# Decoder layer on one core: the recurrence's work in another order on all engines, and TensorE's program written out instead of looped

## What is computed

```python
q, k, v = (x @ Wq), (x @ Wk), (x @ Wv)          # each (b, s, H, HD)
fg = jax.nn.sigmoid(x @ Wf + bf)
def step(state, inp):
    qt, kt, vt, gt = inp
    state = state * gt[..., None] + vt[..., None] * kt[..., None, :]
    out_t = jnp.einsum('bhij,bhj->bhi', state, qt)
    return (state, out_t)
_, outs = jax.lax.scan(step, state0, (qs, ks_, vs, gs))
```

## Time and profile before

| | |
|---|---|
| median of 3 runs | 2022.22 us (2022.18 to 2028.58) |
| the profiled execution | 2018.74 us, span 2016.6 us |
| TensorE products, busy | 1864.5 us (92%), 28151 |
| TensorE weight loads, busy | 1307.0 us (65%), 28151 |
| VectorE, busy | 1593.3 us (79%) |
| ScalarE, busy | 1221.4 us (61%) |
| GpSimd, busy | 390.4 us (19%) |
| instruction DMA (queue 8) | 162 packets, 2.65 MB |

### The profile page before, as it was taken

How to read it: one execution, slowest core, us unless ns; L and a number is a source line. 1 busy time by engine, 2 the same in 40 slices (tenths; PEclk the granted TensorE clock), 3 DMA queues, 4 the chain that set the end, 5 groups by cost and what they waited for, 6 DMA issues and landing times. The chain is left out here.

```text
span 2016.6 us, 71020 instructions
## 1 busy us (share of the span) xinstructions
PE 1864.5 (92%) x28151; PEld 1307.0 (65%) x28151; DVE 1593.3 (79%) x2870; ACT 1221.4 (61%) x2047; POOL 390.4 (19%) x516
## 2 busy tenths in 40 slices
PE   6999999999999977999999999999599988799798
PEld 4666666666666665888888888887344433344687
DVE  6777777777777775888888888887466799998897
ACT  4444554444445434777777777777355666688565
POOL 1111111211111121223232323232100222100121
PEclk9999999999999989999999999999699999999899
DMA  4001100110011001111111111110188788599574
GB/s 126 24 24 29 30 24 24 29 30 24 24 27 32 19 19 63 34 48 32 46 33 46 36 42 38 40 41 7 40 273 267 272 314 312 188 402 409 184 271 148
DMA packets 121324, 205.24 MB, mean 102 GB/s; under 512 B 44851, under 2 KB 98358, under 8 KB 121142
## 3 DMA queue, kind: packets, MB, share of 16 engines
q1 hardware_dynamic: 121142, 202.43, 29.4%
HBM read 108.01 MB, written 85.98 MB: 96 GB/s over the span
## 5 line engine op out<-in xcount | busy, mean ns | idle before, releaser
L1483 PE MATMUL ff_twin<-ff_xq,w_uh 128*128 (+1 forms) x1152 | 346.0, 382 | 40.0 <-DVE ff_top L1852 25.7
L1483 PEld LDWEIGHTS ff_twin<-ff_xq,w_uh 128*128 128x128 f16 x1152 | 110.4, 98 | 188.9 <-issue 43.2
L1483 PE MATMUL ff_twin<-ff_xq,w_ul 128*128 (+1 forms) x576 | 219.9, 382 | 0.0
L1214 DVE TENSOR_REDUCE mneg<-att_s 128x4 f32<-128x512 f32 x256 | 158.8, 683 | 31.3 <-PE att_s L977 31.3
L545 ACT ACTIVATE x<-rec_e,rec_hidden 128x512 f32<-128x512 f32 x256 | 155.8, 702 | 35.1 <-PE rec_e L380 35.1
L661 DVE TENSOR_TENSOR x<-rec_x,rec_until 128x512 f32<-128x512 f32 x256 | 158.7, 681 | 17.2 <-PE rec_x L364 17.2
L392 PE MATMUL rec_x<-x 32*32 32x64 f32 x8192 | 146.4, 219 | 14.9 <-DVE x L661 9.5
L392 PEld LDWEIGHTS rec_x<-x 32*32 32x32 f32 x8192 | 125.4, 107 | 51.4 <-issue 51.3
L288 POOL TENSOR_TENSOR rec_o<-rec_tmp 128x512 f32<-128x512 f32 x32 | 41.1, 1283 | 571.6 <-DVE rec_tmp L714 571.6
L1129 ACT ACTIVATE att_e<-att_s 128x512 f32<-128x512 f32 x256 | 132.2, 612 | 25.4 <-PE att_s L1011 25.4
L349 PE MATMUL rec_f<-rec_xT,w_rec 128*128 128x256 f32 x512 | 137.3, 402 | 0.8 <-ACT rec_v L527 0.8
(11 more groups left out here) (244 smaller groups left out, 4363.3 us busy)
## 6 DMA issues: line engine op xcount, KB each, us to landing
raw_scratch<-ff_out SPq DMA_DIRECT2D x32, 768.0 KB, 3.5
ff_in<-raw_scratch SPq DMA_DIRECT2D x32, 768.0 KB, 5.9
gate_scratch<-ff_out SPq DMA_DIRECT2D x28, 768.0 KB, 3.5
ff_in<-gate_scratch SPq DMA_DIRECT2D x28, 768.0 KB, 10.2
product_scratch<-ff_out SPq DMA_DIRECT2D x28, 768.0 KB, 9.7
ff_out<-product_scratch SPq DMA_DIRECT2D x28, 768.0 KB, 5.9
att_x<-in_x SPq DMA_DIRECT2D x32, 256.0 KB, 2.7
att_ctx<-in_ctx SPq DMA_DIRECT2D x32, 256.0 KB, 3.0
```

What stands on the lines that cost most here:

```text
L1214: V.tensor_reduce(mneg[:, 4 * j:4 * j + 4], X[j].rearrange("p (h k) -> p h k", h=4), AX.X, ALU.max, negate=True).then_inc(q["s_taken"], 1)
L1483: m = T.matmul(bank_.rearrange("p (b n) -> p b n", b=BT), weights(wp, kc, a, c), tile[:, xp, :, kc], start=(i == 0), stop=(i == len(terms) ...
```

## The change

All four compute engines call the recurrence's functions in another order. Step `now` works on three pairs: `prev` is finished, `now` is in its middle, `next_` begins. `Pair` holds a pair's number and buffer; `step(at)` takes the three. On TensorE all small tiles of the pair before stand in one run, quarter and half in turn; scores and whole tiles stand in runs too, and the loop is gone: 34 steps are written out. `across` is split into `keys` and `queries`, the value group of the second sequence comes first, and the weights for q and k get a semaphore of their own, so that the first pair doesn't wait for all four. ScalarE's and VectorE's loops over two steps stay. VectorE takes the quarter products out before the half products, adds the total in the same step, and its work on the weights' scales is cut in three (`weigh_down`, `weigh_up`, `weigh`). The offsets that two semaphores started with are gone. No arithmetic is added or removed.

```diff
-    TURNS = 6
...
+        class Pair:
+            def __init__(self, j, c):
+                self.r, self.s, self.turn = 2 * j + c, c % 2, j + c // 2
+                self.first = isinstance(j, int) and c == 0
...
-                    sp.dma_start(t["w_rec"][:, :, i, :], w[name].rearrange("(c p) d -> p c d", p=P)).then_inc(qw["w_loaded"], 16)
+                    sp.dma_start(t["w_rec"][:, :, i, :], w[name].rearrange("(c p) d -> p c d", p=P)).then_inc(qw["qk_loaded"], 16)
...
-                pool.wait_ge(qw["weighed"], 1)
...
+                            if n == 0:
+                                pool.wait_ge(qw["weighed"], 1)
...
+                def step(at):
+                    prev, now, next_ = at(-1), at(0), at(1)
+                    if prev:
+                        exponents(prev, 4)
+                    if next_:
+                        turn(next_)
+                    if prev:
+                        inside(prev, 0)
+                        inside(prev, 1)
+                        inside(prev, 2)
+                        inside(prev, 3)
+                        across_quarter(prev, 0)
+                        across_half(prev, 0)
+                        across_quarter(prev, 1)
+                        across_half(prev, 1)
+                    if now:
+                        exponents(now, 0)
+                    if next_:
+                        value_gate(next_, 1)
+                    if now:
+                        exponents(now, 1)
+                        scores(now, 0)
+                        exponents(now, 2)
+                    if next_ and not next_.first:
+                        keys(next_, 0)
+                    if next_:
+                        value_gate(next_, 0)
+                    if next_ and next_.first:
+                        keys(next_, 0)
+                    if next_:
+                        keys(next_, 1)
+                    if now:
+                        exponents(now, 3)
+                        scores(now, 1)
+                    if next_:
+                        queries(next_)
...
-                with pe.Fori(0, (NP - 2) // TURNS) as j:
-                    for u in range(TURNS):
-                        p, s = TURNS * j + 1 + u, (1 + u) % 2
-                        pieces(p, s, TURNS // 2 * j + (1 + u) // 2, True, True, True)
-                        products(p + 1, p, 1 - s, s, True, True)
...
+                for p in range(-1, NP + 1):
+                    step(near(0, p))
                 weights()
...
+                def step(at):
+                    prev, now, next_ = at(-1), at(0), at(1)
+                    if prev:
+                        exps(prev, 3)
+                    if now:
+                        gate_exp(now)
+                        if now.first:
+                            gate_log(now)
+                            gate_high(now)
+                        keys_out(now)
+                        if not now.first:
+                            gate_log(now)
+                    if prev:
+                        exps(prev, 4)
+                    if now:
+                        queries_out(now)
+                        if not now.first:
+                            gate_high(now)
+                    if next_:
+                        turned(next_)
+                    if now:
+                        exps(now, 0)
+                    if next_:
+                        values_out(next_, 1)
+                    if now:
+                        exps(now, 1)
+                        exps(now, 2)
+                    if next_:
+                        values_out(next_, 0)
...
-                dve.sem_inc(q["w_ready"], 2)
-                dve.sem_inc(q["o_taken"], TAKES)
...
+                def step(at):
+                    prev, now, next_ = at(-1), at(0), at(1)
+                    if prev:
+                        scores_out(prev, 0)
+                    if now:
+                        floor(now, 0)
+                        if now.first:
+                            weigh_down()
+                    if prev:
+                        weighted(prev, 0)
+                        scores_out(prev, 1)
+                        weighted(prev, 1)
                         for k in range(4):
+                            inside_out(prev, k)
+                    if now:
+                        split(now)
+                        if now.first:
+                            weigh_up()
+                    if prev:
+                        quarter_out(prev)
+                        half_out(prev)
+                    if next_:
+                        floor(next_, 1)
+                    if prev:
+                        total(prev)
+                        if prev.first:
+                            weigh()
```

More of the change, by code:

```diff
@@ L170, in blocks_of, with near, at @@
             return flat.rearrange("p (n q) -> p n q", q=QBLOCK)
[L172 to L182, removed]
+        class Pair:
+            def __init__(self, j, c):
+                self.r, self.s, self.turn = 2 * j + c, c % 2, j + c // 2
+                self.first = isinstance(j, int) and c == 0
+        def near(j, u):
+            def at(k):
+                if isinstance(j, int) and not 0 <= u + k < NP:
+                    return None
+                return Pair(j, u + k)
+            return at
         def rows(j):
@@ L443, in weights @@
                         m.then_inc(qw["turned"], 1)
[L445 to L491, removed]
@@ L517, in turned, with values_out @@
                 def turned(p):
-                    act.wait_ge(q["x_made"], p + 1)
+                    act.wait_ge(q["x_made"], p.r + 1)
                     A.activation(xT.rearrange("p k n -> p (k n)"), F[0][:], ACT.Copy).then_inc(q["xT_ready"], 1)
-                def step(p, s, before, front, back):
-                    if not front:
-                        return
-                    act.wait_ge(q["w_ready"], 2 * p) if not isinstance(p, int) or p else None
-                    for b in range(2):
-                        act.wait_ge(q["z_ready"], 2 * p + b + 1)
-                        A.activation(v[:, s, b * D:(b + 1) * D], F[1 - b][:, 0:D], ACT.Copy).then_inc(q["v_ready"], 1)
+                def values_out(p, b):
+                    if b == 1:
+                        wait_if(act, q["w_ready"], 2 * p.r - 2)
+                    act.wait_ge(q["z_ready"], 2 * p.r + 2 - b)
+                    A.activation(v[:, p.s, b * D:(b + 1) * D], F[1 - b][:, 0:D], ACT.Copy).then_inc(q["v_ready"], 1)
@@ new lines, in exps @@
+                def exps(p, k):
+                    if k == 0:
+                        wait_if(act, q["o_taken"], TAKES * (p.r - 1))
+                    act.wait_ge(q["e_made"], NE * p.r + k + 1)
+                    for asks, r in USES[k]:
+                        out = um[:, p.s, r] if asks else e[:, p.s, r]
+                        A.activation(out, E[(p.s + k) % 2][:], ACT.Exp, bias=hidden[:, asks, r:r + 1] if r < NR else 0.0,
+                                     scale=-1.0 if asks else 1.0).then_inc(q["e_ready"], 1)
@@ L557, in weights @@
                         A.activation(high, W[(WX + i) % len(W)][:], ACT.Copy).then_inc(qw["high"], 1)
-                turned(0)
                 act.wait_ge(q["consts_ready"], 1)
-                steps(act, step)
+                for p in range(-1, 2):
+                    step(near(0, p))
+                with act.Fori(1, NP // 2 - 1) as j:
+                    for u in range(2):
+                        step(near(j, u))
+                for p in range(NP - 2, NP + 1):
+                    step(near(0, p))
                 weights()
@@ L750, in _ @@
+                sums()
+                for p in range(-1, 2):
+                    step(near(0, p))
+                with dve.Fori(1, NP // 2 - 1) as j:
                     for u in range(2):
-                        step(2 * j + 3 + u, (1 + u) % 2, j + 1 + u, True, True)
-                step(NP - 1, 1, (NP - 2) // 2, True, True)
-                step(NP, 0, NP // 2, False, True)
+                        step(near(j, u))
+                for p in range(NP - 2, NP + 1):
+                    step(near(0, p))
```

242 lines of the change are left out of this document (106 added, 136 removed).

## The result

The changed kernel takes 2155.89 us (median of 4 runs, 2149.84 to 2159.72) against 2023.55 beside it: ratio 1.0646, 95% interval 1.0614 to 1.0679. Slower, as forecast, but by 132 us where 33 were forecast; the time lies above the top of the range.

The account below looks back on a forecast made before the run. TensorE was taken to bound the kernel, not VectorE or ScalarE. A step of 19.9 + 3.5 + 0.4 = 23.8 us gave 50 + 29 x 23.8 + 40 = 780 against 745.7, +34.5: 2055 us, range 1998 to 2098.

Parts of the forecast that it names:

- Changes of form, and the wait for VectorE: TensorE's clean step: eight fewer tile-form changes save 1.3 us, the scores' vanished wait 0.63, taking 21.85 to 19.9.
- The loop: TensorE's loop written out: four back edges go, 2.4 us each or 3.2 with a clock fall, about 11 us.
- Code for the dense block: TensorE's small-tile block, 896 instructions, uses packets faster than they come: 3.5 us of stall a step, bounds 0 and 5.0.
- The clock: TensorE's clock falls after idle time: one fall in two steps at 0.8 us, 0.4 a step, bounds 0 and 1.5.
- the ends: First and last steps of the recurrence: first addition at 50 us, last two steps about 20 us each.
- The code keeps up: Rival for TensorE's small-tile block: no stalls, step 19.9 us, 85 us less, 1937 us; chance 0.13.
- half hidden: Rival for TensorE's small-tile block: some 2.0 us of stall, no clock fall, step 21.9, 1997 us; chance 0.12.
- The clock falls at every stall: Rival for TensorE's clock in the recurrence: step 23.4 + 1.5 = 24.9 us, 2087 us; chance 0.10.
- What would show it: Profile signs: interval 23 to 24.5 us, block 10 to 11, stalls one packet apart, TensorE busy time lower, scores' wait gone.

Follow-up runs that it names:

- code_half: The changed kernel with half the instructions for the same columns in the small tiles' inside products, part of the computation left out: 2015.52 us, ratio 0.9981.
- cols_half: The changed kernel with half the columns for the same instructions in the small tiles' inside products, part of the computation left out: 2145.28 us, ratio 1.0618.
- filler_before: The changed kernel with twelve unused fp16 products of 512 columns added ahead of each block of small tiles: 2229.29 us, ratio 1.1026.

## Why the prediction was right in sign and wrong in size

The span's own gain of 131 us against 34.5 forecast, by the steps of the prediction:

1. **and 2. Changes of form, and the wait for VectorE.** A clean step of 19.9 us was forecast. No step of the change is clean; the shortest step in mid-stage without a stall or a fall is 19.93, in `code_half`, which has fewer instructions. The wait is gone, as forecast. Right, as far as it can be read.
3. **The loop.** 11 us forecast for four back edges; 7.9 by taking them out of the old order, and 12 to 17 by putting three into the new one. Right in the main: it is a small term either way.
4. **Code for the dense block.** 3.5 us forecast, 3.1 measured; 2.5 stalls a block forecast, 2.2 measured; 127 products between and 3.7 us a packet. `code_half`, `cols_half` and `filler_before` show that it is the rate of instructions. Right, a little high. The Trainium skill's "mostly hidden" ("Runtime: NRT & Kernel Launch", "Instruction fetch mechanics") isn't borne out for such a block; its advice to write loops out is, by 0.3%.
5. **The clock. This step failed.** It read: one fall in two steps, 0.8 each, 0.4 a step, bounds 0 and 1.5, since "most of a fall hides behind the next stall". Measured: 31 falls in 31 steps. The 29 steps that the sum counts at 23.8 take 26.80 in the mean; less the clean 19.9 and 3.1 of stall, that leaves 3.8. Counted the other way, of 8.4 us at half clock only 0.7 lie in idle time of the array, so next to nothing hides, and half of the other 7.7 is 3.8 as well. So 3.8 us instead of 0.4, 3.4 more in each of 29 steps, 98 us, where the whole forecast lacked 97 (point 4 gives 12 back, the ends take 8, and 2 lie behind the stage). The frequency was wrong by two, the price of a fall by more than four. The 3.8 are two and a half times even the upper bound of 1.5.

Where the price came from: the two back edges in the earlier trace rows. There 2 x 0.20 x 8 = 3.2 us ran at half clock. A block stalls two or three times in a row, and its falls last 8.4 us, into the next value group. The trace of before held such a fall, at the very block that point 4 was taken from the earlier trace rows. Busy time just ahead of and into that block, over it, and behind it, before the change, and TensorE's two waits ahead of it:

```profile
725.00:735.00 10.00, 6.71 (x169) 5.16 (x165) 8.36 (x11) 0.00 (x0) 2.54 (x2) 0.51 0.07 19
731.36:743.83 12.47, 9.32 (x449) 8.98 (x450) 6.34 (x10) 0.00 (x0) 1.33 (x2) 0.77 0.09 25
742.00:749.00 7.00, 5.57 (x38) 5.53 (x38) 3.48 (x6) 2.99 (x5) 1.40 (x2) 0.52 0.01 2
```
```profile
724.52 1.47 PE L364 MATMUL rec_x<-rec_qm,rec_kT 32*128 32x256 f32 x16 [1.98 <-DVE rec_tmp L697]
728.46 2.09 PE L364 MATMUL rec_x<-rec_qm,rec_kT 32*128 32x256 f32 x16 [2.48 <-DVE x L661]
```

The block lasts 12.47 us, where 6.9 of work and 0.86 + 2.29 of stall make 10.05; the 2.4 left are the clock. But the trace's record of the clock has two falls here, and they must be told apart. The first lasts from 725.2 to 735.4. It starts before the block and its stalls, between the two waits for VectorE shown here, and takes in 4.1 us of the block. The prediction saw that the first 256 products took 5.70 us instead of 4.4 and put that down to slower demand for code; it was this half clock. The second fall, from 742.3 to 749.1, stands behind the block's own stalls. Of its 6.8 us 1.1 lie in the last stall, and half of the other 5.7 is 2.8. Had these rows been asked for, one fall in each step at that price would have given 19.9 + 3.5 + 2.8 = 26.2 us a step and about 2125 us (an estimate), above the range and much nearer to the 2156.

*The ends.* The first addition came at 51.99 (50 forecast); the last step took 21.93 and the one before it 23.64 (20 each).

*The rivals.* "The code keeps up" and "half hidden" would have needed stalls of 0 and 2.0 us; they are 3.1. "The clock falls at every stall" came nearest with 0.10. It is one fall a block, not one for each of its two or three stalls, and at 1.5 a step it too was priced from the back edges: 2087 against 2156. The range's upper bound fell with the same price. It was also added up too low: stalls of 5.0 and a clock of 0.7 make a step of 25.6 and some 2107 us, not 2085, and three stalls with nothing hidden are 3 x 1.8 = 5.4 us, not 5.0.

*What would show it.* The stalls, their spacing (3.28 to 4.09, wider than 3.7 to 3.9), the 127 products and the vanished wait stood as said. The interval (26.54, not 23 to 24.5), the block (12.0, not 10 to 11) and TensorE's busy time (up, not down) did not: the three that depend on the clock.

## What to carry to other kernels

Count instructions per microsecond, not only work: 896 instructions in 7 us of small tiles outran a supply of 256 every 3.7 us, whatever their columns. When a stall of the array is forecast, price the clock behind it from a stretch with the same pattern of stalls, by asking for the granted clock of that stretch and of those ahead of and behind it, so that each fall is put down to the right wait; here it cost 3.8 us a step where the stalls cost 3.1. And before a wait is removed, name what the released engine asks for next: covering 0.63 us bought 0.2 in the mean step (0.4 in a clean one), and covering the next wait as well bought nothing that the time shows.

## What was not expected of the hardware

- Adding 12 products a step to TensorE made the kernel 61 us faster, 2155.9 to 2094.7, by keeping the granted clock at 0.97 instead of 0.84.
- Blocks with two or three stalls, 3.1 us together and none over 2.4, came each with 8.4 us at 1.2 GHz in the mean, nearly all of it with the array at work. The back edges of one loop brought 3.2 us of half clock one time and none another; what decides in between, these runs do not tell.
- A stall for code ended 1.2 to 1.6 us after the packet itself had been moved, in 68 cases of 68.
- In `cols_half` the block's columns fell by two fifths (19,456 to 11,264) and a step by 0.1 us (26.42 for 26.54): idle time grew from 97 to 115 us in its place.
